# Layer norm rows of a graph attention kernel: turned by one transposing DMA a batch as fp16 parts, in place of fp32 turns by TensorE

## What is computed

```python
h = jnp.maximum(_layernorm(x, axis=-1), 0.0)      # (x - mean) / sqrt(var + 1e-5), then relu
q, k, v = (split_heads(h @ W.T) for W in (Wq, Wk, Wv))      # 16 heads of 32
a = jnp.einsum('bhnd,bhmd->bhnm', q, k) * D ** (-0.5) + (adj + adj)[:, None]
...
p = jax.nn.softmax(a, axis=-1)
o = jnp.einsum('bhnm,bhmd->bhnd', p, v)
return x + o.transpose(0, 2, 1, 3).reshape(B, N, D) @ Wo.T
```

## Time and profile before

| | |
|---|---|
| median of 3 runs | 1005.39 us (1004.05 to 1005.59) |
| the profiled execution | 1005.16 us |
| its span in the profile | 1003.4 us, 33752 instructions |
| PE busy | 959.6 us (96%) |
| ACT busy | 934.5 us (93%) |
| POOL busy | 862.3 us (86%) |
| DVE busy | 850.0 us (85%) |
| bytes moved by DMA | 183.62 MB |

### The profile page before, as it was taken

One profiled execution on the slowest core, in us unless ns is written; L12 is line 12 of the kernel. 1 busy time (PEld: TensorE's weight loads), 2 busy tenths in 40 slices (PEclk: granted clock), 3 DMA queues, 4 the chain that ended last, 5 costly groups with the idle time before them and its releaser, 6 DMA issues.

```text
span 1003.4 us, 33752 instructions
## 1 busy us (share of the span) xinstructions
PE 959.6 (96%) x11580; PEld 660.2 (66%) x11580; DVE 850.0 (85%) x3092; ACT 934.5 (93%) x3049; POOL 862.3 (86%) x936
## 2 busy tenths in 40 slices
PE   5879999999999999999999999999999999999965
PEld 4656776666677666777666677766666776667632
DVE  6778998888989888898988889988889898888863
ACT  5799999999999999999999999999999999999992
POOL 2278998989998898999888899989889988889894
PEclk9989999999999999999999999999999999999979
DMA  6289999999999999999999999999999999999995
GB/s 251 49 148 195 183 190 194 183 193 186 190 191 184 195 178 187 194 199 180 192 177 198 183 203 184 189 194 178 198 183 197 186 191 193 177 185 176 175 175 119
DMA packets 573818, 183.62 MB, mean 183 GB/s; under 512 B 547024, under 2 KB 555216, under 8 KB 573648
## 3 DMA queue, kind: packets, MB, share of 16 engines
q1 hardware_dynamic: 573648, 181.48, 100.9%
HBM read 29.36 MB, written 16.78 MB: 46 GB/s over the span
## 4 chain that ended last, share of the span: by engine, by line
PE 56%; DVE 28%; issue 8%; ACT 5%; POOL 1%; DMA 1%; DVEq 0%; POOLq 0%; ACTq 0%; SPq 0%
PE ps L1045 35%; DVE logits L752 15%; PE ps L1113 9%; PE ps L1063 7%; DVE stats L649 4%; ACT probs L547 3%; PE ps L942 3%; DVE q_lo L815 2%; DVE o_norm L782 2%; PE ps L1089 1%; DVE some L770 1%; ACT p L560 1%; PE ps L1019 1%; DMA w_nat<-in_L_gnn_Wq 1%; DVE row_min L752 1%
## 5 line engine op out<-in xcount | busy, mean ns | idle before, releaser
L430 POOL TENSOR_TENSOR p<-probs,p 128x512 f16<-128x512 f32 x512 | 586.4, 1161 | 89.9 <-ACT p L560 89.7
L547 ACT ACTIVATE probs<-logits,row_min 128x256 f32<-128x256 f32 x1024 | 513.6, 511 | 3.8 <-DVE row_min L752 3.8
L752 DVE CUSTOM_DVE_ANT_0 logits<-ps,adj_s,sigma 128x256 f32<-128x256 f32 x1024 | 438.0, 475 | 7.1 <-PE ps L1063 7.0
L560 ACT ACTIVATE p<-probs 128x512 f16<-128x512 f32 x512 | 323.5, 632 | 0.0
L1045 PE MATMUL ps<-ht_hi,w_hi 128*128 128x256 f16 x1024 | 280.2, 274 | 7.7 <-DVE q_lo L815 2.6
L1045 PE MATMUL ps<-ht_lo,w_hi 128*128 128x256 f16 x1024 | 279.4, 273 | 0.0
L1045 PE MATMUL ps<-ht_hi,w_lo 128*128 128x256 f16 x1024 | 279.4, 273 | 0.0
L547 ACT ACTIVATION_READ_ACCUMULATOR probs<-logits,row_min 128x1 f32 x1024 | 209.8, 205 | 0.0
L1045 PE MATMUL ps<-wo,o_hi 128*128 128x512 f16 x496 | 149.2, 383 | 3.8 <-POOL o_lo L456 3.8
L1045 PEld LDWEIGHTS ps<-ht_hi,w_hi 128*128 128x128 f16 x1024 | 100.1, 98 | 36.1 <-DVE q_lo L815 13.0
L1045 PEld LDWEIGHTS ps<-ht_lo,w_hi 128*128 128x128 f16 x1024 | 100.4, 98 | 14.0
(11 more groups left out here) (90 smaller groups left out, 1571.0 us busy)
## 6 DMA issues: line engine op xcount, KB each, us to landing
xs<-in_x SPq DMA_DIRECT2D x32, 512.0 KB, 4.6
out<-xs SPq DMA_DIRECT2D x64, 256.0 KB, 2.9
adj_raw<-in_adj SPq DMA_DIRECT2D x32, 256.0 KB, 3.2
pt<-p SPq DMA_TRANSPOSE x256, 4.0
w_nat<-p SPq DMA_TRANSPOSE x256, 3.4
w_nat<-in_L_gnn_Wq SPq DMA_DIRECT2D x2, 512.0 KB, 5.4
w_nat<-in_L_gnn_Wk SPq DMA_DIRECT2D x1, 1024.0 KB, 8.3
w_nat<-in_L_gnn_Wv SPq DMA_DIRECT2D x1, 1024.0 KB, 11.3
```

The costliest lines, as they stand in the source:

```text
L430: g.tensor_tensor(p16[:, c % 2, k, 1], probs[:, h % 4].rearrange("p u n -> p (u n)"), p16[:, c % 2, k, 0], ALU.subtract).then_inc(p_split, 1)
L547: e = a.activation(probs[:, h % 4, u, :], logits[:, h % 4, u, :], ACT.Exp, bias=row_min[:, t.par(d), u, h:h + 1], scale=-1.0, accum_out=ro ...
L560: a.activation(p16[:, c % 2, k, 0], probs[:, h % 4].rearrange("p u n -> p (u n)"), ACT.Copy)\
L752: v.tensor_tensor_reduce(out=logits[:, h % 4, u, :], in0=ps[:, S_BANK + h % HC, N * u:N * u + N], in1=adj_s[:, t.par(d), u, :], scale=sigm ...
```

## The change

Batches 0 to 2 go as before, except that PE turns one row half (128 rows, all 512 features) at a time instead of two feature chunks of both halves. For batches 3 to 31 (`H_TURNED = 3`), 29 of them:

- POOL's `layernorm` makes max(x - mean, 0) without the factor rstd. Multiplication by the positive rstd comes later.
- At step 5 ACT rounds row half 0 and POOL row half 1: xn * rstd to fp16, into `h16`, a part of the weights' store that is free after the start (`round_h`).
- At steps 6 and 10 DVE makes the low parts, xn * rstd - high, into `h16` (`rest_of_h`).
- At step 11 SP waits for both and issues one transposing DMA of 128x2048 fp16 from `h16` to `ht`.
- PE's `turn_h`, ACT's and DVE's `take_h` are gone for these batches. PE's `project` of job 0 waits for the DMA.

For all batches `neg_mean` is gone, since POOL subtracts the mean itself, and `var_s` moves from DVE to POOL, ahead of rstd, with a wait of POOL for its own result. `ht_hi` and `ht_lo` become one tensor `ht`, indexed by row half, part and chunk. The diff, cut to its core:

```diff
+H_TURNED = 3
+H_BY_ACT = (0,)
+H_HI_STEPS, H_LO_STEPS = (5, 5), (6, 10)
...
+        h16 = w16[:, 2]
...
-        ht_hi = sb("ht_hi", [P, 2, NC, N], F16)
-        ht_lo = sb("ht_lo", [P, 2, NC, N], F16)
+        ht = sb("ht", [P, 2, NU, 2 * NC, P], F16)
...
+        def h_rows_free(eng, b):
+
+            if b == H_TURNED:
+                eng.wait_ge(wo16_in, 16 * NC)
+            else:
+                eng.wait_ge(ht_in, 16 * (b - H_TURNED))
...
+                    if s == 11 and later(t, 2) and h_by_dma(t.batch(2)):
+                        b = t.batch(2)
+                        sp.wait_ge(h_split, NU * (b - H_TURNED + 1))
+
+                        sp.wait_ge(pj_full, NJ * t.batch(0) + 6)
+                        sp.dma_start_transpose(ht[:, b % 2].rearrange("p u l n -> p (u l) n"),
+                                               h16[:, 0:NU].rearrange("p u n -> p (u n)")).then_inc(ht_in, 16)
...
             def layernorm(t, d):
 
-                pool.wait_ge(ln_stats, NU * (t.batch(d) + 1))
+                b = t.batch(d)
+                pool.wait_ge(stat_step, 2 * NU * (b + 1))
+                if h_by_dma(b - 1):
+
+                    pool.wait_ge(h_split, NU * (b - H_TURNED))
+                g.tensor_scalar(var_s[:], mean_var[:, :, 1], EPS, 2.0 ** (-2 * H_UP), ALU.add, ALU.mult)\
+                 .then_inc(var_ready, 1)
+                pool.wait_ge(var_ready, b + 1)
                 g.tensor_tensor(rstd[:], var_s[:], minus_half[:], ALU.pow).then_inc(rstd_ready, 1)
-                pool.wait_ge(rstd_ready, t.batch(d) + 1)
-                if d == 2:
-
-                    pool.wait_ge(aux_full, aux_after("h", t.batch(1), 1))
+                if not h_by_dma(b):
+                    pool.wait_ge(rstd_ready, b + 1)
+                if d == 2 and not h_by_dma(b - 1):
+
+                    pool.wait_ge(aux_full, aux_after("h", b - 1, 1))
                 for u in range(NU):
-                    g.tensor_scalar(xn[:, u, :], xs[:, t.batch(d) % X_RING, u, :], neg_mean[:, u:u + 1],
-                                    rstd[:, u:u + 1], ALU.add, ALU.mult).then_inc(xn_ready, 1)
+                    if h_by_dma(b):
+                        g.tensor_scalar(xn[:, u, :], xs[:, b % X_RING, u, :], mean_var[:, u, 0:1], 0.0,
+                                        ALU.subtract, ALU.max).then_inc(xn_ready, 1)
+                    else:
+                        g.tensor_scalar(xn[:, u, :], xs[:, b % X_RING, u, :], mean_var[:, u, 0:1],
+                                        rstd[:, u:u + 1], ALU.subtract, ALU.mult).then_inc(xn_ready, 1)
+
+            def round_h(b, u):
+
+                pool.wait_ge(xn_ready, NU * b + u + 1)
+                pool.wait_ge(rstd_ready, b + 1)
+                h_rows_free(pool, b)
+                g.tensor_scalar(h16[:, u, 0:D], xn[:, u, :], rstd[:, u:u + 1], 1.0, ALU.mult, ALU.mult)\
+                 .then_inc(h_hi_pool, 1)
...
+            def round_h(b, u):
+
+                act.wait_ge(xn_ready, NU * b + u + 1)
+                act.wait_ge(rstd_ready, b + 1)
+                h_rows_free(act, b)
+                a.activation(h16[:, u, 0:D], xn[:, u, :], ACT.Copy, scale=rstd[:, u:u + 1]).then_inc(h_hi_act, 1)
...
-                dve.wait_ge(stat_step, step + 2 * NU)
-                v.tensor_scalar(neg_mean[:], mean_var[:, :, 0], -1.0, None, ALU.mult).then_inc(ln_stats, 1)
-                v.tensor_scalar(var_s[:], mean_var[:, :, 1], EPS, 2.0 ** (-2 * H_UP), ALU.add, ALU.mult)\
-                 .then_inc(ln_stats, 1)
...
+            def rest_of_h(b, u):
+
+                n = b - H_TURNED
+                if u in H_BY_ACT:
+                    dve.wait_ge(h_hi_act, len(H_BY_ACT) * n + H_BY_ACT.index(u) + 1)
+                else:
+                    dve.wait_ge(h_hi_pool, (NU - len(H_BY_ACT)) * n + u - len(H_BY_ACT) + 1)
+                v.scalar_tensor_tensor(out=h16[:, u, D:2 * D], in0=xn[:, u, :], scalar=rstd[:, u:u + 1],
+                                       in1=h16[:, u, 0:D], op0=ALU.mult, op1=ALU.subtract).then_inc(h_split, 1)
...
-                    if j == 0:
+                    if j == 0 and h_by_dma(t.batch(1)):
+
+                        pe.wait_ge(ht_in, 16 * (t.batch(1) - H_TURNED + 1))
+                    elif j == 0:
 
                         pe.wait_ge(aux_taken, aux_after("h", t.batch(1), 1))
```

More of the change, by code:

```diff
@@ L172, in emit @@
         stat_step = sem("stat_step")
-        ln_stats = sem("ln_stats")
+        var_ready = sem("var_ready")
+        h_hi_act = sem("h_hi_act")
+        h_hi_pool = sem("h_hi_pool")
+        h_split = sem("h_split")
+        ht_in = sem("ht_in")
         rstd_ready = sem("rstd_ready")
@@ L230, in emit @@
             for at, key in sorted(slot_uses):
+                if key[0] == "h" and h_by_dma(key[1]):
+                    continue
                 if 0 <= key[1] < NB and not (key[0] == "y" and key[2] not in Y_C):
@@ L304, in h_turns, with h_parts @@
             at = (10, 13) if t.first else (5, 8)
-            return [k for k in range(2) if at[k] == s and later(t, 2)]
+            return [k for k in range(2) if at[k] == s and later(t, 2) and not h_by_dma(t.batch(2))]
         def h_rests(t, s):
             at = (10, 13) if t.first else (6, 10)
-            return [k for k in range(2) if at[k] == s and later(t, 2)]
+            return [k for k in range(2) if at[k] == s and later(t, 2) and not h_by_dma(t.batch(2))]
+        def h_parts(t, s, steps):
+            return [u for u in range(NU) if steps[u] == s and later(t, 2) and h_by_dma(t.batch(2))]
+        def h_rows_free(eng, b):
[3 more added lines that the diff above has]
+                eng.wait_ge(ht_in, 16 * (b - H_TURNED))
         first = Slot(0, -1, False, False, True)
@@ L485, in slot @@
                         layernorm(t, 2)
+                    for u in h_parts(t, s, H_HI_STEPS):
+                        if u not in H_BY_ACT:
+                            round_h(t.batch(2), u)
                     if s == 7 and t.nxt:
@@ L652, in ln_mean_var @@
                 step = 2 * NU * t.batch(d)
+                need(dve, xn_ready, NU * t.batch(d))
                 for u in range(NU):
@@ L862, in slot @@
                             take_h(t.batch(2), k)
+                        for u in h_parts(t, s, H_LO_STEPS):
+                            rest_of_h(t.batch(2), u)
                     for b, u in residuals(t, s):
@@ L939, in turn_h @@
                     need(pe, aux_taken, aux_before("h", b, k))
-                for c in range(2):
-                    for u in range(NU):
-                        m = tr(ps[:, bank, N * c + P * u:N * c + P * u + P],
-                               xn[:, u, P * (2 * k + c):P * (2 * k + c) + P], ident[:])
+                for c in range(NC):
+                    m = tr(ps[:, bank, P * c:P * c + P], xn[:, k, P * c:P * c + P], ident[:])
                 m.then_inc(aux_full, 1)
```

18 lines of the change are left out of this document (9 added, 9 removed).

## The result

The changed kernel takes **1101.38 us** (median of 4 runs, 1099.57 to 1104.93), the kernel before in the same comparison 1005.36 (4 runs, 1004.05 to 1005.59). The ratio is 1.0962, 95% interval 1.0948 to 1.0975: 96 us slower, 96 / 29 = 3.3 us a slot. The forecast was 988, its range ended at 1006, and no rival reached beyond 1046.

The account below looks back on a forecast made before the run. PE and ACT were taken to set the pace, with POOL to become the bound: 28.7 us plus 0.2 gives a 28.9 us slot, saving 0.6 from 29.50, times 29 slots -17.4 us: 988 us, range 969 to 1006.

Parts of the forecast that it names:

- the part on POOL: POOL's work per slot: 27.1 + 0.7 changed instructions + 1.0 meeting DVE - 0.1 = 28.7 us, the most loaded engine.
- a floor and a ceiling as var_s had them: var_s on POOL, absent from the trace: floor k_diag's 0.22 us, ceiling rstd's 0.70; taken as +0.3 (0.2 to 0.8).
- the part on SP and the DMA: SP's queue: 20 us of issue a slot, h's DMA adding 2.5 and landing after 5 us (4 to 9).
- Weakest place: Path from head 10's rounding through h's DMA to q on ACT: 1.3 us of slack, lateness counted at nothing.
- planned extra load: POOL's added work at steps 5 to 10: 1.6 us more, in a shorter slot, making its gaps vanish.
- rival 4: h's DMA lands late, so PE's job 0 and ACT's q wait; up to 1046 us, chance 0.12, of it 0.08 slower.
- DVE "has room": DVE has 3.6 us of room a slot, so gains or losses of half a microsecond there don't count.
- the exclusion: DVE's two low parts of h and POOL's SBUF instructions make each other wait: +1.0 us a slot on POOL (0 to 1.5).
- the signs named for it: Slot 28.9 us, POOL waiting under 0.6, ACT waiting at the split, rest_of_h median over 1 us, POOL instructions stretched about 0.5.
- Rounding and var_s: Instructions added to POOL each slot: rounding of one row half +0.65 us, var_s +0.3 us.
- the 997 for a POOL of 29.2: Time if DVE and POOL exclude each other for the whole instruction: 1.5 us a slot, POOL 29.2, near 997 us.
- the 0.2 of unevenness: ACT waiting for POOL at the split because POOL's load is not smooth: 0.2 us added, a slot of 28.9 us.

Follow-up runs that it names:

- fast xn: Changed kernel with DVE's neg_mean back and POOL's xn as add and multiply by 1.0 for batches 3 to 31, relu left out: 1033.51 us.
- the best form: Whole path rebuilt: POOL xn add and multiply, ACT both high parts with relu, DVE maximum in low parts, neg_mean and var_s, DMA at step 9: 1024.55 us.

## Why the prediction was wrong

**Where the 96 us come from**, as a chain of runs from before to after. The steps interact (early issue is worth 6.1 us or 27.5), so another order would share them out differently:

| step | us | time |
|---|---|---|
| before | | 1005.3 |
| one more transposing DMA a slot | +17.8 | 1023.1 |
| rest of the new path with fast xn, DMA at step 9 | +4.3 | 1027.4 |
| DMA at step 11 | +6.1 | 1033.5 |
| xn with a maximum, batches 3 to 31 | +59.0 | 1092.5 |
| subtraction in place of addition, dear in batches 0 to 2 only, and no neg_mean on DVE | +8.9 | 1101.4 |

**The step that failed first** is in the part on POOL: "xn takes one pointer scalar instead of two, 0.76 to 0.68 each: -0.15". It measured 1.99 each, +2.5 a slot. I priced the instruction by shape and operands and took for granted that add, subtract and maximum cost the same. No row of before has a POOL tensor_scalar with a subtraction or maximum, so it needed a floor and a ceiling as var_s had them, and it got a small gain with no upper end. The subtraction in the earlier trace rows is a TENSOR_TENSOR, 1.16 us, another kind of instruction; even that row would have been a warning. The Trainium skill says in GPSIMD Engine Reference, Elementwise — side-by-side cycle accounting, that 512 elements take 768 ns at best. The traces here don't bear that out as a best time: add and multiply take 0.77 us with two pointers, but 0.70 with a constant, and o_hi of before, of the same shape, takes 618 ns. With a subtraction or maximum it is 1.98 to 2.08 us.

**The second that failed** is the part on SP and the DMA: "16 x 1.26 = 20 us of issue a slot, so 2.5 more fit", and that the heads queued behind step 11 slip by up to 2.5 us, which is covered. I had taken the median of one kind of head; the means of before are 1.38 and 1.49 us, so 23.0 us a slot, and with x, adj and outputs SP is issuing for 25.3 of 29.5 us, counted over 24 slots. With h's turn in every slot and no slow xn it is 27.9 to 28.6 of 30.1 to 30.5, and where SP's queue sets the pace a head waits in it for 4.8 to 5.3 us in the mean, at every step and not behind one. Nor is an issue a fixed price, as the issue moved to ACT shows. The forecast left 9 us of room; the kernel before has 2.9 us a slot in gaps of SP over 0.2 us. Every kernel here with one such h DMA in each slot has a mean slot of 30.1 us or more, whoever does the rest. The 17.8 us alone turn the forecast's gain of 17.4 into nothing. The Trainium skill says in Advanced Engine Details and Errata, X-Bar Transpose (TRN2), that transposing DMAs are as fast as regular ones. The runs here differ from it: the same 512 KB land after 5.4 us turned and 3.5 us copied, in the median, and added to a loaded stream the two forms differ by 18.3 us of the whole time.

**"Weakest place"**: I named h's lateness, found 1.3 us of slack, and counted it at nothing, saying that a POOL that lags by 1 us nearly uses it up. POOL lagged by 2.2 us at head 10's split, and still by 1.7 with the fast xn, so not by the first reason alone: its planned extra load is enough. As rival 4 it had 0.12 and wanted a landing of 7.6, or 6.6 with a lag of 1; it came at 5.2, through the lag. Mechanism right, trigger missed.

**DVE "has room"** held in the changed kernel (26.74 of 31.90) but not behind it: with the fast xn and early DMA, DVE is busy 29.15 of 30.30. I had charged the exclusion to the two low parts and to POOL, not to DVE's small instructions. The chain of before has 28% on DVE, which its busy time alone did not tell me.

**What held.** POOL became the bound, and the load comes out once xn is mended. Of the signs named for it, the low parts of h have a median of 1.02 us, adj_s beside one is stretched by 0.40 us (687 to 1087 ns) and ACT waits for POOL at the split. The exclusion, taken as 1.0 from one row against 1.5 by the rule, measured 0.93. Rounding and var_s are 0.70 and 0.19 against 0.65 and 0.3; landing 5.2 against 5; ACT 28.3 to 28.5 against 28.2. The saving of a slot without PE's turns is there: 29.06 us in most slots when h is copied, and in each second one when it is turned by DMA every second time. What the change was worth at best by these runs is the 5 us of the last one.

**Slips in the sums**, none of which moved the forecast: with rival 4's own formula a landing of 7.6 with the lag stalls for 2.3 us, a slot of 30.5 (the 1.3 and 29.5 belong to 7.6 without it); and the 997 for a POOL of 29.2 leaves out the 0.2 of unevenness, with which it is 1002.

**Still open**: what makes the transposing issues so long. The runs exclude the bytes, and taking the plain issues off SP did not help; between the number of small pieces, the queue behind SP and the hardware that turns them nothing here decides. A copy in as many small pieces, or the added transposition with the plain DMAs on ACT, was not run. The slots of 30.4 us in the run with h copied are not explained either. That the chip could do the best form with a faster transposing stream is argued from that run, not shown.

## What to carry to other kernels

Price an instruction by its operation as well as its shape and operands: where the profile has no row of just that operation on that engine, it has no price, and a few of them behind the last output of any kernel give one. Give each kind of DMA that shares a queue an account of its own, in means, before adding to it; here the bytes said nothing. And where a full replacement runs into a second resource, replace part: every second batch was faster than all and than none.

## What the hardware did unexpectedly

- On POOL, a tensor_scalar over 128x512 fp32 takes 0.70 to 0.77 us with add and multiply, 1.98 to 2.08 us with a subtraction or a maximum among its two operations, and two slow operations cost no more than one.
- A transposing DMA of 512 KB once in 29.5 us, unread, costs a kernel with 16 smaller ones 17.8 us; the same bytes copied cost between -0.8 and +1.1 us by the interval of their ratio.
- A transposing issue on SP is not a fixed price: with four plain DMAs a slot taken off SP, the mean of one kind went from 1.42 to 1.75 us, and SP stayed covered for 28.6 of 30.4 us, with 0.3 us in gaps over 0.2.
- A DVE instruction over 8 elements a row (`some`) has a minimum of 103 to 105 ns, but a mean of 277 ns before, 488 after and 706 in the run with fast xn and early DMA. All those over 0.2 us (65, 94 and 91 of 128) end within 0.03 us of the end of a POOL instruction: they wait for POOL. How long depends on which POOL instruction they meet, and not on how busy POOL is (31.10 of 31.90 us after, 28.42 of 30.30 in the run with 706).
